# Gathers of two expert batches paced by finished units, with the combining moved along, in a graph layer and mixture-of-experts kernel on one core

## The reference

```
msg     = layernorm(x) @ W + B
weights = where(adj < 1, exp(-(1/adj - 1)**2 / (2 * 0.5**2)), 0)
x       = x + weights @ msg

z       = layernorm(x)
top2    = top_k(z @ gate_w + gate_b, 2);  share = softmax(top2 values)
h       = relu(z @ w1[e] + b1[e]);  expert_out = h @ w2[e] + b2[e]
y       = z + sum over the two of share * expert_out
x       = x + layernorm(y) * gamma + beta
```

## Time and profile before

| | us |
|---|---|
| median of three timed runs | 1702.58 |
| lowest and highest | 1701.91, 1702.87 |
| span of the profiled execution | 1823.2 |

### The profile page before, as it was taken

One profiled execution on the slowest core, in us unless ns is written; L12 is line 12 of the kernel. 1 busy time (PEld: TensorE's weight loads), 2 busy tenths in 40 slices (PEclk: granted clock), 3 DMA queues, 4 the chain that ended last, 5 costly groups with the idle time before them and its releaser, 6 DMA issues.

```text
span 1823.2 us, 24195 instructions
## 1 busy us (share of the span) xinstructions
PE 1624.7 (89%) x8178; PEld 1073.6 (59%) x8178; DVE 1499.7 (82%) x2298; ACT 1565.7 (86%) x1502; POOL 463.6 (25%) x342
## 2 busy tenths in 40 slices
PE   4999999999999999999999999999999987384720
PEld 3666666666666666666666656666666786373620
DVE  7999998989899999999999989999998443153464
ACT  5899999999999999999999999999999664253531
POOL 0001223131314040407132231313140213535342
PEclk9999999999999999999999999999999999696765
DMA  9559867676767676776776676787673244343431
GB/s 313 158 160 290 235 199 215 195 217 193 214 195 212 196 212 198 220 213 202 210 202 209 199 210 199 209 247 208 202 206 121 80 124 143 87 141 97 129 110 50
DMA packets 216792, 338.22 MB, mean 186 GB/s; under 512 B 18080, under 2 KB 74144, under 8 KB 216544
## 3 DMA queue, kind: packets, MB, share of 16 engines
q1 hardware_dynamic: 208368, 319.62, 59.8%
q0 software_dynamic: 8304, 17.06, 3.1%
HBM read 303.07 MB, written 33.55 MB: 185 GB/s over the span
## 4 chain that ended last, share of the span: by engine, by line
PE 84%; DVE 6%; another core or an unknown queue 5%; issue 3%; ACT 1%; DMA 1%; DVEq 0%; SPq 0%; ACTq 0%
PE acc L1118 48%; PE tp L1137 24%; PE tp L1164 4%; PE tp L1192 3%; PE acc L1192 2%; DVE chunk L654 1%; PE tp L1153 1%; DVE stats L666 1%; DVE chunk L660 1%; DVE chunk L1004 1%; PE misc L1094 1%; ACT chunk L613 1%; DVE msg L729 1%; DMA xs<-in_x_dram 1%
## 5 line engine op out<-in xcount | busy, mean ns | idle before, releaser
L1118 PE MATMUL acc<-wT,msg 128*128 128x512 f32 x2048 | 976.0, 599 | 0.0
L527 ACT ACTIVATE wT<-tp 128x1024 f32<-128x1024 f32 x512 | 761.0, 1674 | 14.0 <-PE tp L1137 12.4
L521 ACT ACTIVATE chunk<-chunk 128x2048 f32<-128x2048 f32 x256 | 655.3, 2560 | 0.1
L660 DVE SCALAR_TENSOR_TENSOR chunk<-chunk 128x2048 f32<-128x2048 f32 x256 | 584.8, 2284 | 54.7 <-ACT chunk L521 54.1
L1137 PEld LDWEIGHTS tp<-ident,chunk 128*128 128x128 f32 x4096 | 478.7, 141 | 223.2 <-issue 221.5
L654 DVE SCALAR_TENSOR_TENSOR chunk<-chunk 128x2048 f32<-128x2048 f32 x256 | 583.5, 2280 | 1.9 <-DMA chunk<-in_adj_dram 1.9
L1137 PE MATMUL tp<-ident,chunk 128*128 128x128 f32 x4096 | 534.3, 274 | 0.0
L516 ACT ACTIVATE chunk<-chunk 128x4096 f32<-128x4096 f32 x118 | 511.0, 4331 | 0.0
L1118 PEld LDWEIGHTS acc<-wT,msg 128*128 128x128 f32 x2048 | 349.1, 190 | 258.3 <-issue 245.8
L457 POOL TENSOR_TENSOR pool_carrier<-pool_carrier 1x1 f32<-1x1 f32 x32 | 43.7, 1365 | 951.5 <-DVE row_now L845 825.9
L476 POOL DMA_INDIRECT rows_in<-y,row_now x128 | 216.7, 1693 | 40.4 <-issue 40.4
(11 more groups left out here) (121 smaller groups left out, 794.7 us busy)
## 6 DMA issues: line engine op xcount, KB each, us to landing
chunk<-in_adj_dram SPq DMA_DIRECT2D x256, 1024.0 KB, 5.4
chunk<-rows_in SPq DMA_DIRECT2D x118, 64.0 KB
rows_out<-chunk SPq DMA_DIRECT2D x59, 128.0 KB
chunk<-rows_in SPq DMA_DIRECT2D x35, 128.0 KB
rows_out<-chunk SPq DMA_DIRECT2D x17, 256.0 KB
y_kept<-y SPq DMA_DIRECT2D x16, 256.0 KB, 6.1
chunk<-y_kept SPq DMA_DIRECT2D x16, 256.0 KB
out_dram<-chunk SPq DMA_DIRECT2D x16, 256.0 KB
```

The costliest lines, as they stand in the source:

```text
L521: act.activation(slot(c), slot(c), ACT.Exp, scale=-1.0).then_inc(inverted, 1)
L527: act.activation(wT[:, (g * PPG + m) % WSLOTS, :], tp[(g * PPG + m) % TSLOTS][:, :], ACT.Exp, scale=-2.0).then_inc(weighted, 1)
L660: dve.scalar_tensor_tensor(out=slot(c), in0=slot(c), scalar=2.0, in1=slot(c), op0=ALU.subtract, op1=ALU.mult).then_inc(squared, 1)
L1118: ins = pe.matmul(acc[:, :], msg[:, n, :], wT[:, (g * PPG + m) % WSLOTS, k * ROWS:(k + 1) * ROWS], start=(n == 0), stop=(n == 2 * PPG - 1))
```

## The change

Two things change. First, POOL waits before each gather of groups 0 to 8, and before the first four of group 9, until a stated number of units has had its bias added (`ro_ready`). The numbers come from a count of tiles: each gather is due 1.5 tiles after the one before it, and not before the batch's last tile plus 4. A due time past the last tile of all gets no wait. Second, `starts` follows from it: a group's combining may start 4 tiles after its last gather is due, and always at least 11 iterations after the group before it; the pace of 6 among the units of two tiles is gone. The load of the normalized rows stays six iterations ahead of the start.

```diff
-        COMBINE_WAIT, COMBINE_PACE, COMBINE_LONG = 8, 6, 11
-        starts = []
+        COMBINE_LONG, LOAD_Z_AHEAD = 11, 6
+        GATHER_PACE, RESULTS_LATE, LANDED = 1.5, 4, 4
+        tiles_done = [0]
+        for u in range(NU):
+            tiles_done.append(tiles_done[-1] + TILES[batch_of(u)])
+
+        def units_at(t):
+
+            return sum(d < t for d in tiles_done)
+
+        gather_after, starts = {}, []
+        t = 0
         for b, n in enumerate(BATCHES):
-            for _ in range(n):
-                at = UNIT0[b + 1] + COMBINE_WAIT
-                pace = COMBINE_PACE if starts and UR[batch_of(starts[-1])] > P else COMBINE_LONG
-                starts.append(max(at, starts[-1] + pace) if starts else at)
+            for g in range(FIRST[b], FIRST[b + 1]):
+                for kb in range(KB):
+                    t = max(t + GATHER_PACE, tiles_done[UNIT0[b + 1]] + RESULTS_LATE)
+                    if t <= tiles_done[-1]:
+                        gather_after[g, kb] = units_at(t)
+                at = units_at(t + LANDED)
+                starts.append(max(at, starts[-1] + COMBINE_LONG) if starts else at)
         LAST = starts[-1] + COMBINE_LONG + 2
@@
-                    if i == starts[g] - COMBINE_PACE:
+                    if i == starts[g] - LOAD_Z_AHEAD:
                         load_z(g)
@@
                     carry()
                     for kb in range(KB):
+                        if (g, kb) in gather_after:
+                            pool.wait_ge(ro_ready, gather_after[g, kb])
                         pool.indirect_dma_start(
```

## The result

The changed kernel takes 1718.38 us (median of four runs, 1718.07 to 1718.78), the kernel before beside it 1702.72. The ratio is 1.0089, with a 95% interval of 1.0075 to 1.0104: slower, by 15.7 us. So about 1.8 us of the prediction's 11.3 lie around the span, and the rest must be something else.

What follows compares the result with a forecast made beforehand. Engines bound the first part, PE the second batch, DVE's combining the end after the last unit. 1702.6 + 20.0 for moved combining - 2 for stall = 1720.6 us, other terms 0; range 1693 to 1728.

Steps and rivals of the forecast that it cites:

- the prediction's 11.3: Tail: median timed run of 1702.6 us minus the 1691.3 us sum, the most stall a timed run could contain.
- the 2 us taken off for a stall: Tail: part of the 0 to 11.3 us of possible timed stall that waits between gathers would give back.
- The moved combining: After the last unit: rest of group 6 and nine groups, 78.4 us in place of 58.4, so 20.0 us more.
- What comes back among the units: Second and third batches: PE is the bound, so taking combining off DVE there gains 0, at most 11.4 us.
- DVE's wait for group 0: Second batch, kernel before: DVE waits 2.6 us for gathers, PE's two banks cover 3.9 us, removing it brings nothing.
- The stall belongs to the profiled execution: Tail: of 131.9 us of profiled stall at most 11.3 are in timed runs; the profiled execution has the rest.
- (b): Tail: burst stall is real in timed runs and pacing removes 30 us of it, giving 1692.6 us; chance 0.19.
- The sum of 1691.3 us for a free tail: End of span at free pace: 1435.3 + 74.5 + 69.0 + 51.3 + 58.4 + 2.8 us, against a profiled 1823.2.
- The gathers at the end: After the last unit: group 15's rows land at about 58 us, asked for at 70.0; nobody waits, cost 0.
- (c): POOL: waits never bind, only the moved starts act, 1722.6 us; chance 0.56 together with the forecast.
- (d): Among the units: waits bind too hard, gathers, units and DVE wait in a circle, 14 us, about 1735; chance 0.04.
- (a): Tail: as forecast, but all of the 11.3 us is stall and goes, 1711.3 us; chance 0.14.

Runs made afterwards that it cites:

- half of the move: Kernel before with combining starts 8 iterations apart in place of 6 among the units of two tiles, no waits; 1713.18 us, ratio 1.0057.
- the overlapped end: Kernel before with groups starting 6 iterations apart in place of 11 once the units are over; 1706.12 us, ratio 1.0017.

## Why the prediction was right

The forecast was 1720.6 us, the time is 1718.4, and the mechanism of its main term is the one it named. The closeness is in part luck: the 2 us taken off for a stall, which timed runs do not have, stood in for 5.2 us that came back among the units and were put at 0. Several other steps were wrong without moving the sum. The signs it named are there: nine starts 8.43 us apart after the last unit, the eight gathers of each of groups 0 to 4 in 11.7 to 12.0 us, and PE busy for 1199.68 us of 200 to 1400.

- **The moved combining, +20.0 us: right.** After the last bias come 82.0 us against 61.6, +20.4. With the starts alone the time is the same, and with half of the move it is +9.0 for one more group.
- **What comes back among the units, 0, with 2 for the stall: mis-sized.** From unit 71 to the last bias the changed kernel takes 118.6 us, the kernel before 123.9: 5.2 come back. By stretches: units 71 to 85, 27.7 against 29.7 us, 2.0 less; 85 to 103, 35.3 both times, so combining at a pace of 6 among the units of two tiles is free, as predicted; 103 to 109, 7.4 against 9.4, 2.0 less, where the kernel before still has groups at the close pace while the units change to one tile; from there to the last bias 1.2 less. The rest, 0.7, lies in the first part. 20.4 - 5.2 - 0.7 = 14.5, the difference of the spans.
- **DVE's wait for group 0 costs nothing: wrong.** The prediction saw it, 2.6 us, and let PE's two banks hide it with 3.9 us of cover. It is 4.25 us long in the clean profile, and 2.0 us of it remain at unit 85. The landing was taken too short: 1.1 us by a gather whose data moved while the DMA engines were otherwise idle, where group 0's rows are there 3.8 us after the last issue, with the DMA engines 0.96 busy. The cover was taken too long as well. With the overlapped end DVE waits 3.54 us at this place and units 71 to 85 take 28.9 us, with the pace of 8 it is 3.67 and 29.1; against the 27.7 us of the kernels whose wait is 1.25 us or less, 2.2 to 2.3 us are hidden each time. An estimate agrees: behind its wait DVE does four share instructions (1.18 us) and the bias (0.42) before PE gets its bank back, and 3.9 - 1.6 = 2.3. The changed kernel waits at group 0 too, 1.25 us after 4.2 us of landing, where the prediction had 1.8 us of slack; the cover hides it.
- **The stall belongs to the profiled execution because something in profiling does it: wrong.** The bound of 11.3 us on what a timed run can contain was sound and carried the forecast against rival (b). But the same kernel profiled again shows no such stall, and neither does the kernel with the moved starts and no waits, with its bursts of gathers. It was one disturbed execution.
- **The sum of 1691.3 us for a free tail: 10.5 too low.** The clean span is 1701.8. In pieces that overlap by some tenths of a us, the last 18 units of the first batch, with the change to tiles of two, take 23.0 us from the bias of unit 53 to that of unit 71, where I put 18.0. The second batch takes 71.1 for 69.0, the third 52.8 from its first bias to its last for 50.1 at 1.09, the end 61.6 for 61.2, and unit 0 comes 0.7 later. So the 11.3 us were 1.8 around the span and paces taken where they run best, 2.0 of them DVE's wait for group 0. The 2 us for the stall had no ground.
- **The gathers at the end, 12 us of slack: wrong, at no cost.** The slack without waits is 9.9 us. With them it is gone, since POOL is held back and begins group 10 only 6.8 us after the last bias, where I had it begin group 11 by then. The chains happened to end together. The runs with 1.75 tiles and with the pace of 6 put back show what the next step costs: 13 us, and all that the earlier combining would have brought.
- **The rivals.** (c) is true in its effect and not in its reason: the waits do bind, and hold the last gather back by 10 us, but they change no time beside those starts. (d) is real as a mechanism where starts leave no lead, 40.6 us among the units and 19.2 at the end in the run with the waits alone; the changed kernel escapes it through its later starts. (a) falls with its stall, and (b) falls: no run with waits is faster.

## What to carry to other kernels

Work that has to be done anyway is cheap only while another engine covers it. Count what a new order leaves for the time after the cover ends, and take its pitch from there. Then set up the chain of every engine that must run through, here POOL's 128 gathers at 1.3 us each: a pacing wait on it costs nothing until its slack is used up, and one for one from there on. How long rows take to arrive is to be read where the DMA engines are as busy as they will be there, not in an idle stretch. A profile whose span is far from the time should be taken again before a cause is read out of it.

## What the runs showed of the hardware that I had not expected

- One execution of a kernel on one core had 121 us of stall spread over its tail, with PE, ACT and DVE idle for most of its worst 40 us and the DMA engines 0.28 busy, while POOL went on issuing; the next profile of the same kernel had none. The cause stays open.
- With no units running it takes 1.6 to 1.8 us (in one case 3.0) from the end of a group's last issue on POOL to the start of the DVE instruction that waits for its rows, for example 1.65 in the changed kernel (1703.43 to 1705.08), for 128 rows of 512 bytes. Among the units it was 3.8 us for group 0 in the kernel before and 4.2 in the changed kernel. Of the 1.65 us about 1.1 are over when the data have moved (by 1704.5). The Trainium skill ("DMA: Bandwidth & Descriptors", the section on the anatomy of a SWDGE transfer) gives about 2.0 us for the fixed part, most of it after the last byte. The trace agrees that the end of the data is not yet the signal, but only about 0.6 us lie behind it here, and from the start of the issue to DVE's start it is 2.6 us.
- Eight gathers on POOL are not equally long everywhere: 10.1 us inside the stall, where DVE did next to nothing, 10.46 in the mean of the kernel before, 11.0 to 11.5 with the overlapped end. In the twelve profiles 86 issues take over 1.2 us in place of 0.95, and 84 of them overlap one of DVE's two steps on 128x512 (gamma and the added row). That these steps lengthen the issues is likely and was not tested by a run.
